# GELU evaluated twice, the final stage's constants loaded ahead, and the sign setup moved into the first projections

## The reference, cut to what matters

```python
x = x + attn_a(layernorm(x))        # 16 heads, softmax times a decay, projection
x = x + ffn(layernorm(x))
x = x + attn_b(layernorm(x))        # biased q, k, v; output y = o @ Wo + bo is layer-normed, * gamma + beta
x = x + ffn(layernorm(x))

def ffn(x):                         # w1: (1024, 256), w2: (256, 1024)
    alpha = mean(abs(w), axis=1, keepdims=True)      # for w1 and for w2
    h = gelu(x @ (alpha1 * sign(w1)).T + b1, approximate=False)
    return h @ (alpha2 * sign(w2)).T + b2
```

## Time and profile before

| | |
|---|---|
| device time, median of 2 runs | 2498.24 us (2497.08 to 2499.41) |
| device time of the profiled execution | 2501.24 us |
| its span, first to last instruction | 2499.5 us |
| mean granted clock of TensorE | 0.951 of full speed |
| busy: PE, DVE, ACT, POOL | 2300.7, 1896.7, 1474.9, 1028.5 us |
| busy share of PE in the 40 slices | 7 to 9 tenths, but for 0 to 2 at the start and 4 to 5 where stages meet |

### The profile page before, as it was taken

The page is one execution under the profiler, slowest core; times in us unless marked ns, Lnnn a source line. Parts: engine busy times, 40 slices in busy tenths (PEclk is TensorE's granted clock), DMA queues, the critical chain, the costliest instruction groups (busy, mean ns, idle before and its releaser), DMA issues. The chain is left out here.

```text
span 2499.5 us, 49776 instructions
## 1 busy us (share of the span) xinstructions
PE 2300.7 (92%) x16288; PEld 1332.6 (53%) x16288; DVE 1896.7 (76%) x4787; ACT 1474.9 (59%) x3293; POOL 1028.5 (41%) x1309
## 2 busy tenths in 40 slices
PE   4979999999999999879996899999999999995887
PEld 2545555555555545467764555454554545544666
DVE  5668988888788889156653898888888988914886
ACT  1228687787868787423331357777777777671333
POOL 0038789789888977922211101010010100014542
PEclk8979999999999999989998789999999999996999
DMA  4662122130312211144324511130321303113211
GB/s 150 254 177 70 33 65 64 39 87 20 81 41 57 72 29 41 35 132 150 128 91 130 120 32 52 46 91 25 77 57 40 91 28 74 40 36 120 68 43 34
DMA packets 162095, 188.69 MB, mean 75 GB/s; under 512 B 69552, under 2 KB 92848, under 8 KB 161072
## 3 DMA queue, kind: packets, MB, share of 16 engines
q1 hardware_dynamic: 160496, 180.26, 25.0%
q10 hardware_dynamic: 1344, 5.24, 0.6%
HBM read 114.37 MB, written 69.99 MB: 74 GB/s over the span
## 5 line engine op out<-in xcount | busy, mean ns | idle before, releaser
L919 POOL TENSOR_TENSOR att_a_wd<-att_a_wt,decay 128x256 f32<-128x256 f32 (+3 forms) x896 | 749.8, 874 | 139.4 <-ACT att_a_wt L946 109.9
L946 ACT ACTIVATE att_b_wt<-att_b_ps 128x512 f32<-128x512 f32 (+3 forms) x1280 | 590.8, 540 | 251.1 <-PE att_b_ps L1070 245.9
L987 DVE TENSOR_REDUCE att_b_mpart<-att_b_pm 128x1 f32<-128x512 f32 x768 | 495.8, 684 | 77.6 <-PE att_b_pm L1050 76.2
L987 DVE TENSOR_REDUCE att_a_mpart<-att_a_pm 128x1 f32<-128x512 f32 x768 | 498.3, 683 | 69.9 <-PE att_a_pm L1050 67.3
L946 ACT ACTIVATE att_a_wt<-att_a_ps 128x512 f32<-128x512 f32 (+3 forms) x896 | 412.1, 512 | 169.4 <-PE att_a_ps L1070 166.3
L929 POOL TENSOR_SCALAR_AFFINE_SELECT att_b_wt<-att_b_wt 128x512 f32<-128x512 f32 x128 | 81.2, 635 | 782.2 <-ACT att_b_wt L946 782.2
L1070 PE MATMUL att_b_ps<-att_b_mx,ones_row 64*128 64x512 f32 (+3 forms) x1280 | 372.0, 368 | 0.0
L1063 PE MATMUL att_b_ps<-att_b_qop,att_b_kop 64*128 64x512 f32 (+3 forms) x1024 | 331.5, 425 | 2.0 <-ACT att_b_wt L946 0.9
L1050 PE MATMUL att_a_pm<-att_a_kop,att_a_qop 64*128 64x512 f32 (+3 forms) x1024 | 316.4, 427 | 14.0 <-ACT att_a_pm L952 7.9
L1050 PE MATMUL att_b_pm<-att_b_kop,att_b_qop 64*128 64x512 f32 (+3 forms) x1024 | 298.5, 387 | 2.0 <-DVE att_b_mpart L991 1.0
L1098 PE MATMUL att_b_po<-att_b_wt,att_b_va 128*17 128x512 f32 (+3 forms) x2560 | 294.0, 536 | 0.0
(11 more groups left out here) (185 smaller groups left out, 3509.4 us busy)
## 6 DMA issues: line engine op xcount, KB each, us to landing
att_a_kop<-qk SPq DMA_DIRECT2D x224, 64.0 KB, 2.9
att_b_kop<-qk SPq DMA_DIRECT2D x224, 64.0 KB, 2.9
att_a_qop<-qk SPq DMA_DIRECT2D x216, 64.0 KB, 3.0
att_b_qop<-qk SPq DMA_DIRECT2D x216, 64.0 KB, 3.0
qk<-qkv_a_qk_hi SPq DMA_DIRECT2D x8, 1024.0 KB, 4.0
qk<-qkv_a_qk_lo SPq DMA_DIRECT2D x8, 1024.0 KB, 6.4
y<-att_a_y SPq DMA_DIRECT2D x32, 256.0 KB, 2.2
y_ahead<-y SPq DMA_DIRECT2D x32, 256.0 KB
```

The lines of the kernel that those rows point to most:

```text
L919: pool.tensor_tensor(wd[:, v % WD, h, a:z], wt[:, v % buffers, h, a:z], keep["decay"][:, u:u + z - a], ALU.mult).then_inc(w_decayed, 1)
L946: act.activation(wt[:, v % buffers, h, a:CH], pe_[:, n % EBANKS, 0:CH - a], ACT.Exp)\
L987: dve.tensor_reduce(mpart[:, g % 2, c, piece, u:u + 1], pm[:, n % MBANKS, 0:w], AX.X, ALU.max, negate=True).then_inc(m_reduced, 1)
```

## The change

Three things are changed.

**1. The setup stage is gone.** Its work is inside the projections. ACT issues the load of w1 after its first square root, then waits for w_scaled and for w1's landing before it issues that of w2, and only then goes on to the first copy of the transposed x. DVE does the sign work after chunks 0 to 3 (alpha or signs, w1 then w2). PE transposes the signs 8 at a time at the start of chunks 4 to 7, in the PSUM tile of v, behind a new wait for DVE's copy of the v before; ACT copies them out. SP stores `w1s` ahead of chunk 6's stores and `w2s` ahead of chunk 7's. The loop over the two sequences is written out.

```diff
+    act.dma_start(w1...).then_inc(w_loaded, 16)            # ACT, after root(0, 0)
     act.wait_ge(w_scaled, 1)
+    act.wait_ge(w_loaded, 16)
+    act.dma_start(w2...).then_inc(w_loaded, 16)
...
+    if G == 0:                                             # ACT, after root of the next chunk
+        act.dma_start(decay); act.dma_start(b1); act.dma_start(b2)
+    if G >= NC:
+        for n in (2 * (G - NC), 2 * (G - NC) + 1):
+            act.wait_ge(w_turned, n + 1)
+            act.activation(to, flat[...], ACT.Copy).then_inc(w_kept, 1)
...
                     finish(b, c)                           # DVE
+                    if b == 0 and c < 2:
+                        sign(w1, sign1, D, HT, keep["alpha1"], 0, c)
+                    if b == 0 and c >= 2:
+                        sign(w2, sign2, FF, KT, keep["alpha2"], 4, c - 2)
...
+                    if G >= NC:                            # PE, start of a chunk
+                        pe.wait_ge(v_kept, G + 1)
+                        turn_signs(G - NC)
...
+                    if NC * b + c == NC + 3:               # SP, behind the 16 small loads
+                        sp.wait_ge(w_kept, 8)
+                        sp.dma_start(dram["w2s"], w2s...).then_inc(signs_out, 16)
                     store(b, c)
```

```diff
-    plan = [("Y", 0), ("P", 0), ("S", 0), ("Y", 1)]
+    plan = [("Y", 0), ("Y", 1), ("P", 0), ("S", 0)]
     if not qkv:
         plan += [("A", 0), ("N", 0)]
     plan += [("P", 1), ("S", 1), ("X", 0)]
-    if not qkv:
-        plan += [("A", 1), ("N", 1), ("Y", 2)]
-    plan += [("H", 0, h) for h in range(EARLY)]
+    between = [[] for h in range(EARLY)] if qkv else [[("A", 1)], [("N", 1)], [("Y", 2)]]
+    for h in range(EARLY):
+        plan += [("H", 0, h)] + between[h]
```

```diff
-    act.activation(g[:, h % GB, :], ph[:, BANK[item], :], ACT.Gelu, ...).then_inc(g_ready, 1)
+    for dst, ready in ((g_hi[:, h % GB, :], g_hi_ready), (ph[:, BANK[item], :], g_ready)):
+        act.activation(dst, ph[:, BANK[item], :], ACT.Gelu, ...).then_inc(ready, 1)
...
-    dve.tensor_copy(g_hi[:, h % GB, :], g[:, h % GB, :]).then_inc(g_hi_ready, 1)
-    dve.tensor_tensor(g_lo[:, h % GB, :], g[:, h % GB, :], g_hi[...], ALU.subtract)
+    dve.tensor_tensor(g_lo[:, h % GB, :], ph[:, BANK[item], :], g_hi[...], ALU.subtract)
...
-    pe.wait_ge(g_ready, HT * G + n + 1)        # H: its bank is free
+    pe.wait_ge(g_lo_ready, HT * G + n + 1)
...
-    pe.wait_ge(g_lo_ready, HT * G + h + 1)     # O, for all four matmuls
+    for part, ready in ((g_hi, g_hi_ready), (g_lo, g_lo_ready)):
+        pe.wait_ge(ready, HT * G + h + 1)
```

More of the change, by code:

```diff
@@ L221, in halves_variance, with projections @@
                                     op0=ALU.mult, op1=ALU.add)
-def projections(nc, name, x_dram, weights, biases, v_ones, keep, dram):
+def projections(nc, name, x_dram, weights, biases, v_ones, ffn, keep, dram):
     with ExitStack() as ctx:
@@ L299, in body @@
                         load_first_chunk(sp, keep, dram, first_in)
+                    if NC * b + c == NC + 2:
+                        sp.wait_ge(w_kept, 4)
+                        sp.dma_start(dram["w1s"], w1s[:, :, :].bitcast(F32)).then_inc(signs_out, 16)
+                    if NC * b + c == NC + 3:
+                        sp.wait_ge(w_kept, 8)
+                        sp.dma_start(dram["w2s"], w2s[:, :, :].bitcast(F32)).then_inc(signs_out, 16)
                     store(b, c)
-            sequences(sp, body)
+            for b in range(B):
+                body(b, b == B - 1)
             sp.wait_ge(first_in, FIRST_LOADS)
+            sp.wait_ge(const_loaded, 48)
+            sp.wait_ge(signs_out, 32)
             for par in range(2):
@@ L375, in _ @@
                 dve.wait_ge(vt_filled, 2)
-            sequences(dve, body)
+            for b in range(B):
+                body(b, b == B - 1)
         @block.scalar
@@ L405, in _ @@
             root(0, 0)
+            act.dma_start(w1[:, :, :], ffn["w1"].rearrange("(t p) d -> p t d", p=P)).then_inc(w_loaded, 16)
             act.wait_ge(w_scaled, 1)
-            sequences(act, body)
+            act.wait_ge(w_loaded, 16)
+            act.dma_start(w2[:, :, :], ffn["w2"].rearrange("(t p) d -> p t d", p=P)).then_inc(w_loaded, 16)
+            for b in range(B):
+                body(b, b == B - 1)
         @block.tensor
@@ L445, in _ @@
             pe.wait_ge(w_scaled, 1)
-            sequences(pe, body)
+            for b in range(B):
+                body(b, b == B - 1)
 UNITS = GH * TB
@@ L582, in score @@
         if k == 0 and (c, kb) == (sequence(g)[0], near(c, self.decayed)[0]) and g == GROUPS - 1:
[L583 to L584 removed]
+            for i in range(NEXT if self.decayed else NEXT + 3):
+                self.soon(self.issued + 4000.0 + 3600.0 * i, "N", g, i)
         self.items.append(("S", g, self.scores, c, kb, HEADS[k]))
@@ L724, in next_loads, with attention @@
                           dram["inverse"][0, c, heads, :].unsqueeze(1).to_broadcast([H // KT, HD, CH])))
-        for k in range(TB):
-            loads.append((keep["x"][c][:, k, :], at(x_src, 0, c)[:, k, :]))
     return loads
-def attention(nc, name, decayed, x_src, w, keep, dram):
+def attention(nc, name, decayed, x_src, w, norm, keep, dram):
     with ExitStack() as ctx:
@@ L1218, in dense @@
         if norm:
-            bo, gamma, beta = (sb(n, [P, D], F32) for n in ("bo", "gamma", "beta"))
+            bo, gamma, beta = (keep["norm"][:, i, :] for i in range(3))
             z, zn, zg = (sb(n, [P, TB, D], F32) for n in ("z", "zn", "zg"))
@@ L1654, in build @@
               [t[f"L0_attn_b_b{n}"] for n in "qkv"], keep, scratch)
-        attention(nc, "att_b", False, x[1], t["L0_attn_b_Wo"], keep, scratch)
-        dense(nc, "end", x[1], x[2], [t[f"L0_attn_b_{n}"] for n in ("bo", "gamma", "beta")],
+        attention(nc, "att_b", False, x[1], t["L0_attn_b_Wo"], [t[f"L0_attn_b_{n}"] for n in ("bo", "gamma", "beta")], keep, scratch)
+        dense(nc, "end", x[1], x[2], True,
               None, None, keep, scratch)
```

243 lines of the change are left out of this document (102 added, 141 removed).

## The result

| | before | changed |
|---|---|---|
| device time, median | 2498.24 us | 2459.11 us (2457.01 to 2461.20, 2 runs) |
| ratio to before | | 0.984, 95% interval 0.980 to 0.989 |
| profiled execution: time, span | 2501.24, 2499.5 us | 2461.20, 2458.5 us |
| granted clock of TensorE, mean | 0.951 | 0.955 |

The change is 1.6% faster, 39 us where 35 were forecast. Four more executions of it, beside seven of before in another set of runs, gave 2456.88 us and a ratio of 0.984 (0.982 to 0.985).

A forecast was written before the change was run, and what follows sets the result against it. TensorE bounds projections (VectorE close behind) and dense mid; dense end has slack, paying for waits and lost clock. Projections −4.7, dense mid −2.5, dense end −27.9 sum to −35.1: 2466.1 us profiled, 2463 median, range 2442 to 2484.

The forecast's parts named there:

- x at once, and w1's landing: Setup and projections: x loaded at about 0.8 instead of 34.10 us, −33.3; ACT's first copy waits for w1, +2.8.
- Sign work, clock and sign transposes: Projections: uncovered VectorE sign work +12.2, TensorE's lower clock in chunks 0 to 3 +6.8, extra transposes on PE +4.2.
- Tail: End of the projections: SP puts the 1 MB store of w2s ahead of the last three stores, +2.6 us.
- Attention a: First attention stage: TensorE's order unchanged, only three more small loads in the attention stages, so ±1 us.
- Dense mid: Middle dense stage: head −3.5 as the second P starts earlier, body 0, bank wait tenths +1; −2.5 us in all.
- Dense end's head: Start of the last dense stage: beta ahead −4.1, zg on DVE −1.1, two xb's +1, first O −3.7; together −7.9 us.
- Dense end's body: Last dense stage: shorter waits for g_lo and the residual and P's clock, −4.0 in each of five periods, −20 us.
- the second rival: Dense end's body: GpSimd still stretches subtractions out of PSUM, only the cast's −1.5 per period remains, −7.5 not −20; chance 0.13.
- more comes of it: Projections keep their clock and dense end's period nears 21: −53 us, about 2445; chance 0.14.
- POOL still blocks DVE: Dense end: zg and xb stretch PSUM subtractions too, waits stay, −7.5 instead of −20; 2476 us; chance 0.13.
- The projections give it all back: Projections: low clock over the whole 6.1 us of chunks 0 to 3, +24 instead of +6.8; 2480 us; chance 0.12.
- The bank: Dense stages: in-place second GELU in PSUM beyond 0.4 us slack costs 12.8 us per 0.1; 2527 at 1.65; chance 0.04.

The follow-up runs named there:

- e8: Changed kernel, but SyncE instead of ACT issues the loads of w1, w2, decay, b1 and b2, behind those of x; median 2452.71 us, ratio 0.981.
- e4: Changed kernel, but the second GELU writes g in SBUF instead of the PSUM bank, so g_lo has two SBUF inputs; median 2463.91 us, ratio 0.988.
- e3: Kernel before, plus only the constants loaded ahead and the new order of first work, with old GELU and old setup; median 2482.97 us, ratio 0.994.
- e1: Kernel before, with only the setup's move into the projections; median 2496.27 us, ratio 0.999.
- e7: Changed kernel, but the first O of a chunk takes po's two halves in turn, each behind ACT's copy of that half; median 2454.39 us, ratio 0.982.
- e9: Changed kernel, with one more 128x512 copy on ACT between the two GELUs of each of the 128 blocks; 2477.00 us, one run.

## Why the prediction was right, and where it was not

The total was 4 us off. That is closer than the terms deserve: attention a came out 7 us too long, and the other four stages each gained 2 to 4 us more than forecast.

- **x at once, and w1's landing**: −33.3 + 2.8 = −30.5 forecast; the first q/k product came at 14.31 instead of 45.36, −31.05. The wait for w1 was 1.9 (e8), just under the range's 2.
- **Sign work, clock and sign transposes**: 12.2 + 6.8 + 4.2 = 23.2 forecast; from the first q/k product to the end of the last v it is 23.3 us longer. That near agreement is luck in part. By the waits, the sign work cost 11.1 less the four holes of 0.44, 9.3, since part of chunk 3's lay under the sign transposes. The low clock cost about 5: the periods of chunks 1, 2 and 3 are 3.0, 1.7 and 0.2 us longer than their waits explain. This is the part that changes from one execution to the next: the first four chunks, from the first q/k product to the end of chunk 3's v, take 58.4 to 63.0 us in the nine traces that have the same orders of TensorE and VectorE there, with the same waits for xn, and 61.7 in this one. The granted clock over them is 0.97 in the shortest and 0.92 in the longest and in this one. The transposes and their waits cost 4 × 2.44 less two holes of 0.44, 8.9. The term mis-sized most was the last, 8.9 instead of 4.2: I had covered chunk 4's by the sign work of chunk 3, but VectorE copies v before it does signs, so TensorE waits the 1.51 there too, and chunk 7's was not hidden by the store either.
- **Tail**: +2.6 forecast, −0.3 measured (from the end of the last v to TensorE's first instruction of attention, 11.4 and then 11.1 us). SyncE was through with its 16 loads earlier relative to TensorE's end, so the last stores started earlier than they had and made room for w2s.
- **Attention a**: ±1 forecast, +7 in the trace and about +4 over all traces. This is the step of the prediction that failed: I took the stage to be out of the change's reach because no instruction of its own had moved. In its place the runs show late first loads in all eleven traces with the new stage ahead and a late return of the clock in nine of them; how the stage before brings either about stays open.
- **Dense mid**: −2.5 forecast, −6.1 (−7.1 in the second execution). The body, which I had put at 0, gave 0.7 per chunk in periods of 32.4. The step that failed was to read TensorE's 34.45 of 35 us as a body in which nothing could show: the missing 0.55 held the wait of 0.48 ahead of P, and it is gone. Of the 0.7, 0.6 came with the PSUM source (e4). The head brought the first H 4.0 us earlier but the first o only 0.6 (1.7 in the second execution). With the old GELU (e3) the first o did come 4.2 us earlier. With the new one, H(0,2) waits 0.5 us for its bank, and the H matmuls stay near 0.63 us, where 0.39 is full speed, for 8 us; before, that was so for 3 us of them. So the head's −3.5 was right for the order alone, and the new GELU, which I had priced in the body only, took most of it back.
- **Dense end's head**: −7.9 forecast, −7.1 to the first O (43.1 to 36.0 us from the stage's start), −8.8 in the second execution. z gained 2.8 and not 4.1, since the first P takes 6.62 instead of 5.29 us, nearly all of it at the low clock. That is chance: in the second execution P takes 5.29, and z gains 4.1 as forecast.
- **Dense end's body**: −4.0 per period forecast, −4.4 measured: 2.4 less of waiting and 2.0 less in the length of TensorE's work, by the clock. I had counted two of four waits; a period of before also held 1.07 for `xt_lo` and 0.72 for o. The prediction gave the cast 1.5 of a period (the second rival's −7.5) and the port the rest; e4 gives 3.3, three quarters, to the cast and 1.1 to the port. So the number is right, and the mechanism behind most of it was the smaller one of the two that I had named. The 65 ns that stood against a PSUM source did not show: 688 ns on average, where an undisturbed subtraction with two SBUF inputs takes 693.
- **The rivals**: "more comes of it" named a period near 21. The waits for ACT's o, for `xt_lo` and for the bank, 1.06, 0.79 and 0.36 us of a period, are what lies between that and 22.9. "POOL still blocks DVE" is refuted by 64 subtractions of at most 694 ns. "The projections give it all back" came true in effect for the move alone (e1: 2 us), by another way: not in the projections' clock but in attention a. Its time of 2480 did not. The bank was not the limit in the changed kernel, and its price was wrong: a first copy of 0.52 us costs 18 us, where the slack should have covered it, by ACT's queue and not by the bank; only the second brings the bank in, in dense mid.

## What to carry to other kernels

An operation taken off a busy engine's queue pays twice where TensorE's waits for it had also cost it its clock (2.4 and 2.0 us of a period here); look at the length of the next block of matmuls to see whether it did. When work is hidden inside a stage, ask which of its engines has the least in hand and where on that engine's chain the work is put: the sign work cost TensorE 9 us of waits on VectorE, ahead of the statistics, and some 2 with the signs on GpSimd and the alphas behind VectorE's last copy of v. Time added to an engine with idle time to spare can still cost: ask what else stands behind it in the same queue. A stage none of whose instructions moved can still change by its first loads and its clock, so read the stages' lengths one by one before a gain is called kept. And take a second trace before a difference of 1 to 5 us in one stage is explained.

## What the runs showed of the hardware that was not expected

- Attention a's first loads of 64 KB land in 3.0 to 3.1 us (median of SyncE's) after the old stage and in 3.7 to 4.0 after the new one, with no load of their own changed. No experiment removed it.
- The same stage with the same waits takes 58.4 to 63.0 us over its first four chunks from one execution to the next. Over them the granted clock is 0.97 in the two shortest (e7, e9) and 0.92 in the longest (e1).
- A tensor-scalar operation of VectorE with its tensor in SBUF took 2.54 us instead of 1.38 for four under GpSimd's work, while the statistics (four BN_STATS) kept their 1.4.
- The contention runs both ways: beside VectorE's subtraction of two SBUF inputs, 11 of GpSimd's 64 scalings of x in dense mid took over 1 us, and none took over 0.57 with the PSUM source.
- ACT's GELU onto its own source in PSUM takes 744 ns, less than the one into SBUF: 781 for `g_hi`, 772 for the second GELU of e4.
